# Turning the inverted chunk rows back while VectorE still works on them, with unread wide products on TensorE in two stages of a four-block kernel

## The chip, the cores and the metric

The kernel runs on one core of a Trainium2 chip. The metric is the device time of one execution in microseconds, the median of several runs. All data are 32-bit floats.

## The reference, cut to what matters

The reference is a chain of four blocks over 4096 tokens of 128 channels (16 sequences of 256): an attention with decays, a two-of-eight expert layer, a delta-rule attention, and a one-of-eight expert layer, each followed by a layer norm over the sum with its input. The change lies in the third block, in its projections and in the inverse of its chunks:

```python
q, k, v = silu(causal_conv(hs @ Wq)), silu(causal_conv(hs @ Wk)), silu(causal_conv(hs @ Wv))
q, k = l2norm(q), l2norm(k)                      # 4 heads of 32 channels
k_beta = k * sigmoid(hs @ Wb)
A = where(strict_lower, -(k_beta @ k.T), 0)      # 32x32, per head and chunk of 32 tokens
for i in range(1, 32):
    row = A[i]
    A[i] = row + row @ A
T = A + eye(32)
u, w = T @ v, T @ k_beta                         # then a scan over the 8 chunks of a sequence
local_long = depthwise_fir(v, firl)              # 63 taps
```

## The kernel before, in words

The program is a row of stages; between most of them all engines meet. The third block is `delta_project`, `delta_invert` and `gate_stage`. The engines run their own instruction lists and wait on semaphores.

`delta_project` takes 8 groups of 512 tokens. For each group TensorE (PE) turns four tiles of normalized rows into channel-major form (L1381, and L1430 for group 0), makes the projections with their convolution as 128x512 products (`convolve`, L1386; the projections of v and of beta, L1398 and L1402), sums squares by head (L1409), and multiplies keys with keys and queries in 128 products of 32x32 by 64 columns (L1422, "scores"). Work is staged one and two groups ahead. In the last group nothing is ahead, so PE has only the square sums and, once VectorE (DVE) has made `kq` (L1644, semaphore `s_kq`), the scores; DVE then masks them into `A` and `attn` (L1576). At the stage's start PE's first instruction is the turning of group 0, tile by tile as DVE normalizes it.

`delta_invert` has all 512 chunk matrices (128 chunks of 4 heads) at once. PE turns `A` so that the 128 partitions are the chunks (32 transposes of 128x128, L1698), ScalarE (ACT) copies them into `M[chunk, row, head, column]` in 8 groups of 4 rows (L1731). DVE then substitutes column by column, for j from 1 to 30:

```python
tmp = M[:, j+1:32, hh, j] * M[:, j, hh, 0:j]     # L1761, two pairs of heads
M[:, j+1:32, hh, 0:j] += tmp                     # L1768
```

These are 4 instructions a step, 120 in all, each of which raises `s_dve` by one. Row i no longer changes after step i-1. While DVE works, PE computes the long FIR in 768 products of 32x32 (L1711), which ACT copies out in 8 parts (L1734, semaphore `s_fc`). After the last step DVE sets the four diagonals to 1 (L1773) and raises `s_done`; PE waits for `s_done`, turns the 32 rows of `M` back (L1721), four to a PSUM bank, and ACT copies the 8 banks over `A` (L1744, semaphore `s_U`), after which `gate_stage` starts with products of 32x32 (L1982, L2013) and copies on GpSimd (POOL, L2213). PE may use a bank again when the copy before has left it (`s_U` at k-3). Between the FIR's copies and L1744, ACT loads two tables and makes three small activations (L1737 to L1740).

Of the kernel before, what the change touches and what calls it, by code (L numbers as in the profile page):

```python
# [22 lines left out]
P = 128  # L23
# [6 lines left out]
NG = TOK // GTOK  # L30
# [1244 lines left out]
def delta_project(nc, sem, keep, x_parts, xT_out, v_rows, s_rows, tables, w):  # L1275
# [10 lines left out]
    with ctx:  # L1286
# [3 lines left out]
        C, wqkv, wb, taps, tapr, fir = (tables[n] for n in ("C", "wqkv", "wb", "taps", "tapr", "fir"))  # L1290
# [22 lines left out]
        B = [ctx.enter_context(nc.psum_tensor(f"c_bank{i}", [P, GTOK], F32))[:, :] for i in range(8)]  # L1313

        def s(name):
            return sem("delta_" + name)

        s_set, s_x, s_out = s("constants_set"), [s("rows_in_0"), s("rows_in_1")], s("rows_out")
        s_T, s_xT, s_p, s_pad, s_beta = s("transposed"), s("channel_major"), s("projected"), s("padded"), s("beta")
# [4 lines left out]
        s_ln, s_dve, s_blk, s_wc = s("logarithms"), s("vector_steps"), s("value_blocks"), s("weights_by_tap")  # L1324
# [3 lines left out]
        block = ctx.enter_context(nc.Block())  # L1328
# [44 lines left out]
        @block.tensor  # L1373
        def _(pe):
            mm = nc.tensor.matmul

            def turn_rows(m):
                pe.wait_ge(s_xT, m)
                for t in range(GT):
                    pe.wait_ge(s_xn, 4 * m + t + 1)  # L1380
                    i = nc.tensor.transpose(B[0][:, t * P:(t + 1) * P], xn[:, t, :], C["ident"])  # L1381
                i.then_inc(s_T, 1)

            def convolve(k):
                for j in range(4):
                    i = mm(B[1 + k].rearrange("p (s t) -> p s t", s=GSEQ), wc[:, k, j, :], xT[:, :, j:SEQ + j],  # L1386
                           start=(j == 0), stop=(j == 3))
                i.then_inc(s_p, 1)

            def project(m, first=False):  # L1390

                rows = xT[:, :, 3:SEQ + 3]
                out = lambda b: B[b].rearrange("p (s t) -> p s t", s=GSEQ)
                pe.wait_ge(s_xT, m + 1)
                convolve(0)
                if not first:
                    pe.wait_ge(s_pad, m)
                mm(out(3), wqkv[:, 2, :], rows, start=True, stop=True).then_inc(s_p, 1)  # L1398
                convolve(1)
                if not first:  # L1400
                    pe.wait_ge(s_beta, m)
                mm(out(4), wb[:], rows, start=True, stop=True).then_inc(s_p, 1)  # L1402

            def step(n, b, r, first, last):
                if not first:
                    pe.wait_ge(s_ln, 2 * n)
                for k in range(2):
                    pe.wait_ge(s_sq, 2 * n + k + 1)
                    mm(B[5 + k], C["same32"], sq[k][:], start=True, stop=True).then_inc(s_ss, 1)  # L1409
                if not first:  # L1410
                    pe.wait_ge(s_m, 2 * n)
                if not last:
                    project(n + 1)
                if ahead(n, 2):
                    turn_rows(n + 2)
                pe.wait_ge(s_kq, n + 1)
                if not last:
                    pe.wait_ge(s_act, 3 * n + 5)
                for c in range(GTOK // 32):
                    for h in range(4):  # L1420
                        rows = slice(32 * h, 32 * h + 32)
                        i = mm(B[1 + c // NCH][rows, (c % NCH) * 64:(c % NCH) * 64 + 64], kn[rows, 32 * c:32 * c + 32],  # L1422
                               kq[rows, c].rearrange("p k c -> p (k c)"), start=True, stop=True,
                               skip_group_check=True)
                    if c % NCH == NCH - 1:
                        i.then_inc(s_sc, 1)

            for t in range(GT):
                pe.wait_ge(s_xn, t + 1)
                i = nc.tensor.transpose(B[0][:, t * P:(t + 1) * P], xn[:, t, :], C["ident"])  # L1430
            i.then_inc(s_T, 1)
            pe.wait_ge(s_wc, 1)
            project(0, first=True)
            turn_rows(1)
            steps(pe, step)
# [221 lines left out]
def delta_invert(nc, sem, keep, l_rows, later, loads):  # L1657
# [4 lines left out]
    with ctx:  # L1662
# [3 lines left out]
        C, toe = {"ident": keep["ident"][:]}, keep["toe"]  # L1666
# [6 lines left out]
        def s(name):  # L1673
            return sem("invert_" + name)

        s_fir, s_fc, s_out, s_later = s("fir"), s("fir_copied"), s("fir_out"), s("gate_weights_in")
        s_at, s_M, s_done, s_ut, s_U, s_dve = s("chunks_transposed"), s("chunk_rows"), s("inverted"), s("back_transposed"), s("kept"), s("vector_steps")
        block = ctx.enter_context(nc.Block())

        @block.sync  # L1680
        def _(sp):
            for dst, src in loads:
                sp.dma_start(dst, src).then_inc(s_later, 16)
            sp.wait_ge(s_fc, 8)
            sp.dma_start(l_rows, fir[:].rearrange("p m c -> p (m c)")).then_inc(s_out, 16)
            sp.wait_ge(s_out, 16)
            sp.wait_ge(keep["value_blocks"], 16)

        @block.tensor
        def _(pe):  # L1690
            mm = nc.tensor.matmul
            A = keep["A"][:].rearrange("p n s c -> p (n s) c")
            V = keep["v"][:].rearrange("p n s c -> p (n s) c")
            for c in range(32):
                k = c // 4
                if c % 4 == 0 and k >= 4:
                    pe.wait_ge(s_M, k - 3)
                i = nc.tensor.transpose(Q[k % 4][:, (c % 4) * P:(c % 4 + 1) * P], A[:, :, c], C["ident"])  # L1698
                if c % 4 == 3:
                    i.then_inc(s_at, 1)  # L1700

            pe.wait_ge(keep["toeplitz_in"], 16)
            for k in range(8):
                if k >= 4:
                    pe.wait_ge(s_fc, k - 3)
                for j in range(4):
                    c = 4 * k + j
                    for lag in range(LAGS):
                        for h in range(4):
                            rows = slice(32 * h, 32 * h + 32)  # L1710
                            i = mm(R[k % 4][rows, j * P + lag * NSEQ:(j + 1) * P], toe[rows, c, lag, :],  # L1711
                                   V[rows, 0:P - lag * NSEQ, c],
                                   start=(j == 0 and lag == 0), stop=(lag == LAGS - 1), skip_group_check=True)
                i.then_inc(s_fir, 1)
            pe.wait_ge(s_done, 1)
            for c in range(32):
                k = c // 4
                pe.wait_ge(s_M, 8)
                if c % 4 == 0 and k >= 4:
                    pe.wait_ge(s_U, k - 3)  # L1720
                i = nc.tensor.transpose(Q[k % 4][:, (c % 4) * P:(c % 4 + 1) * P],  # L1721
                                        M[:, c].rearrange("p h j -> p (h j)"), C["ident"])
                if c % 4 == 3:
                    i.then_inc(s_ut, 1)
# [21 lines left out]
        @block.vector  # L1746
        def _(dve):
            v = nc.vector
            dve.wait_ge(s_M, 8)
            done = [0, 0]  # L1750
            own = Steps(s_dve)


            for j in range(1, 31):
                rows = 31 - j
                for pair in range(2):
                    hh = slice(2 * pair, 2 * pair + 2)
                    t = tmp[pair][:, 0:rows * 2 * j].rearrange("p (i h c) -> p i h c", h=2, c=j)
                    if done[pair]:
                        dve.wait_ge(s_dve, done[pair])  # L1760
                    done[pair] = own.mark(v.tensor_tensor(t, M[:, j + 1:32, hh, j:j + 1].broadcast_to([P, rows, 2, j]),  # L1761
                                                 M[:, j:j + 1, hh, 0:j].broadcast_to([P, rows, 2, j]), ALU.mult))
                for pair in range(2):
                    hh = slice(2 * pair, 2 * pair + 2)
                    out = M[:, j + 1:32, hh, 0:j]
                    t = tmp[pair][:, 0:rows * 2 * j].rearrange("p (i h c) -> p i h c", h=2, c=j)
                    dve.wait_ge(s_dve, done[pair])
                    done[pair] = own.mark(v.tensor_tensor(out, out, t, ALU.add))  # L1768
            dve.wait_ge(s_dve, done[1])
            flat = M[:].rearrange("p i h c -> p (i h c)")  # L1770
            for h in range(4):

                i = v.memset(flat[:, h * 32:h * 32 + 31 * 129 + 1:129], 1.0)  # L1773
            i.then_inc(s_done, 1)


def gate_tables(nc, ctx, w, consts, route):
# [1005 lines left out]
```

## Time and profile before

| | |
|---|---|
| median of 3 runs | 1081.73 us (1079.55 to 1085.17) |
| the profiled execution | 1084.69 us, span 1082.9 us |
| busy share PE, DVE, ACT, POOL | 83%, 68%, 51%, 41% |
| mean granted TensorE clock | 0.894 |
| `delta_project` | about 514 to 657 us |
| `delta_invert` | about 657 to 722 us |

A row of the timeline gives start and duration in us from the span's start, the engine, the line, the operation with what it writes and reads, how many instructions were merged, and in brackets how long the engine was idle before and what ended it. PEld is the weight load of TensorE. In a row of windows the busy time (and number of instructions) of PE, PEld, DVE, ACT and POOL is followed by the granted TensorE clock as a share of 2.4 GHz, the DMA share and GB/s. 0.50 is 1.2 GHz and 1.00 is 2.4 GHz.

### The profile page before, as it was taken

The numbers are of one execution on the slowest core, as the hardware profiler recorded it, in microseconds if no ns is written. First come the engines' busy times: TensorE is split into PE (matmuls) and PEld (weight loads), VectorE is DVE, ScalarE is ACT, GpSimd is POOL, SyncE is SP. The second block draws the span as 40 slices with busy tenths as digits, with TensorE's granted clock in tenths as the row PEclk, the third lists the DMA queues.
The fourth block names the chain that finished last, engine by engine and source line by source line (L and its number), as shares of the span: only waits on it lengthen the run. The fifth ranks groups of instructions, "written<-read, shape, count | busy, mean of one in ns | idle before, by whom it ended". The sixth has DMA issues, their size and how long they took to land. (4 is left out here: it accounts for less than half of the span.)

```text
span 1082.9 us, 34100 instructions
## 1 busy us (share of the span) xinstructions
PE 897.5 (83%) x12739; PEld 642.8 (59%) x12740; DVE 741.6 (68%) x2235; ACT 551.0 (51%) x1103; POOL 444.0 (41%) x576
## 2 busy tenths in 40 slices
PE   7899999999853999996689878849899997519995
PEld 4567666666633888886244437647566663218884
DVE  3778898887543555554588896943689997745664
ACT  1477666666311455543377772333565555316663
POOL 1001333444463445444376640011134544655776
PEclk7899999999965999999699997956899997658998
DMA  3112221153012311111443215123112225012110
GB/s 93 21 41 51 58 54 48 50 187 102 24 50 79 86 53 57 56 55 31 105 101 88 60 31 171 45 74 103 42 52 59 64 72 195 13 50 51 54 54 22
DMA packets 122053, 73.14 MB, mean 68 GB/s; under 512 B 63299, under 2 KB 108457, under 8 KB 121536
## 3 DMA queue, kind: packets, MB, share of 16 engines
q1 hardware_dynamic: 113648, 57.80, 19.8%
q0 software_dynamic: 6592, 12.70, 3.4%
q8 instruction: 93, 1.52, 0.6%
q10 hardware_dynamic: 1680, 0.80, 0.3%
q14 instruction: 40, 0.33, 0.1%
HBM read 42.69 MB, written 27.38 MB: 65 GB/s over the span
## 5 line engine op out<-in xcount | busy, mean ns | idle before, releaser
L1181 ACT ACTIVATE bx_h<-bx_up,bx_cur 128x128 f32<-128x128 f32 x284 | 81.0, 369 | 104.9 <-PE bx_up L1152 98.7
L1110 POOL DMA_INDIRECT chosen_b<-bx_ys,bx_to x71 | 73.6, 1037 | 97.8 <-DVE bx_ys L1224 69.1
L601 POOL DMA_INDIRECT regions_b<-a_xo,a_seat x64 | 65.2, 1019 | 88.7 <-ACT a_at L715 69.6
L715 ACT ACTIVATE a_at<-a_scores 128x1024 f32<-128x1024 f32 x64 | 65.6, 1025 | 69.9 <-PE a_scores L469 63.0
L1152 PE MATMUL bx_up<-bx_xT,bx_cur 128*128 128x128 f32 x568 | 81.3, 287 | 5.5 <-DVE bx_cur L1197 3.9
L1134 PE MATMUL bx_down<-bk_w,bx_h 128*128 x568 | 80.8, 285 | 3.2 <-ACT bx_h L1181 3.2
L1152 PEld LDWEIGHTS bx_up<-bx_xT,bx_cur 128*128 128x128 f32 x568 | 70.3, 195 | 15.2 <-DVE bx_cur L1197 9.5
L1134 PEld LDWEIGHTS bx_down<-bk_w,bx_h 128*128 128x128 f32 x568 | 68.8, 191 | 6.6 <-issue 3.7
L1197 DVE TENSOR_SCALAR bx_cur<-bk_w 128x516 f32 x71 | 30.6, 431 | 53.4 <-issue 49.7
L1386 PE MATMUL c_bank<-c_xT,c_wc 128*128 128x512 f32 x128 | 62.1, 630 | 4.8 <-DVE keep_attn L1576 4.0
L464 PE MATMUL a_scores<-a_rk,a_kx 32*128 32x128 f32 (+3 forms) x1024 | 56.8, 293 | 8.8 <-DVE a_at L928 6.3
L464 PEld LDWEIGHTS a_scores<-a_rk,a_kx 32*128 32x128 f32 x1024 | 42.1, 189 | 35.8 <-DVE a_at L928 27.4
L608 POOL TENSOR_SCALAR a_vr<-a_mv 128x4 f32<-128x4 f32 x8 | 1.9, 242 | 133.8 <-DVE a_mv L867 133.7
L469 PE MATMUL a_scores<-a_rk,a_kx 32*128 32x32 f32 (+3 forms) x1024 | 55.1, 276 | 1.3 <-issue 1.3
L928 DVE COPY_PREDICATED a_at<-a_earlier,a_scores 128x256 f32<-128x256 uint32 x64 | 28.1, 440 | 35.9 <-ACT a_at L715 35.0
L1386 PEld LDWEIGHTS c_bank<-c_xT,c_wc 128*128 128x128 f32 x128 | 25.3, 200 | 39.5 <-issue 32.1
L2213 POOL COPY g_kak<-keep_k 128x512 f32<-128x512 f32 x16 | 9.9, 620 | 93.6 <-POOLq L2731 68.7
L1152 PE MATMUL dx_up<-dx_xT,dx_cur 128*128 128x128 f32 x312 | 46.4, 294 | 0.8 <-issue 0.6
L1170 ACT ACTIVATE dx_cur<-space 128x516 f32 x39 | 24.7, 633 | 41.5 <-ACT dx_h L1181 22.2
L1134 PE MATMUL dx_down<-space,dx_h 128*128 x312 | 45.6, 290 | 0.2 <-ACT dx_h L1181 0.2
L1110 POOL DMA_INDIRECT out_rows<-dx_ys,dx_to x39 | 42.4, 1088 | 7.9 <-issue 7.9
L1181 ACT ACTIVATE dx_h<-dx_up,dx_cur 128x128 f32<-128x128 f32 x156 | 43.9, 363 | 3.2 <-PE dx_up L1152 3.2
(450 smaller groups left out, 2492.8 us busy)
## 6 DMA issues: line engine op xcount, KB each, us to landing
bx_xs<-regions_b SPq DMA_DIRECT2D x72, 65.0 KB, 1.9
bk_w<-in_b_w SPq DMA_DIRECT2D x16, 256.0 KB
space<-in_d_w SPq DMA_DIRECT2D x16, 256.0 KB
c_part<-chosen_b SPq DMA_DIRECT2D x15, 256.0 KB
dx_xs<-regions_d SPq DMA_DIRECT2D x40, 65.0 KB, 1.9
a_xp<-in_a_xT SPq DMA_DIRECT2D x8, 256.0 KB
a_xr<-in_x SPq DMA_DIRECT2D x8, 256.0 KB
lion_values<-a_vt SPq DMA_DIRECT2D x8, 256.0 KB
```

The costliest lines, as they stand in the source:

```text
L464: mm(S4[:, g, o:o + P - 32 * q], kx[rows, 0, 4 * t + q].rearrange("p h j -> p (h j)"), rk[b][rows, 0, t * P + 32 * q:(t + 1) * P], start=T ...
L469: i = mm(S4[:, g, o + P - 32 * q:o + P + 32], kx[rows, 1, 4 * t + q].rearrange("p h j -> p (h j)"), rk[b][rows, 2, t * P:t * P + 32 * q + 32],
L601: nc.gpsimd.indirect_dma_start(route["regions"], bass.IndirectOffsetOnAxis(ap=seat[b][:, k, t:t + 1], axis=0), xo[b][k][:, t, :], None).th ...
L715: op(at[m % 2][:], S4[:, :, 0:320].rearrange("p g (q k) -> p g q k", q=2)[:, :, :, 0:P], ACT.Copy).then_inc(s_ata, 1)
L928: v.copy_predicated(at[m % 2][:, :, :, 0:32], earlier[:].unsqueeze(1).unsqueeze(1).broadcast_to([P, 4, 2, 32]), later).then_inc(s_atd, 1)
L1110: nc.gpsimd.indirect_dma_start(dest, bass.IndirectOffsetOnAxis(ap=to[u][:, 0:1], axis=0), ys[u][:], None, bounds_check=dest.shape[0] - 1, ...
L1134: i = mm(BY[u % 2][:, 0:P], h[u % 2][:, f, :], w2[:, bass.ds(e, 1), f, :].rearrange("p e c -> p (e c)"), start=(f == 0), stop=(f == FC - 1))
L1152: i = mm(BU[u % 2][:, f * P:(f + 1) * P], cur[u % 2][:, f * P:(f + 1) * P], xT[u % 2][:], start=True, stop=True)
L1170: op(cur[u % 2][:], w1[:, bass.ds(e, 1), :].rearrange("p e c -> p (e c)"), ACT.Copy).then_inc(s_cur, 1)
L1181: i = op(h[u % 2][:, f, :], BU[u % 2][:, f * P:(f + 1) * P], act_fn, bias=cur[u % 2][:, FC * P + f:FC * P + f + 1])
L1197: v.tensor_scalar(cur[u % 2][:], w1[:, bass.ds(e, 1), :].rearrange("p e c -> p (e c)"), 1.0, None, ALU.mult).then_inc(s_cur, 1)
L1386: i = mm(B[1 + k].rearrange("p (s t) -> p s t", s=GSEQ), wc[:, k, j, :], xT[:, :, j:SEQ + j], start=(j == 0), stop=(j == 3))
```

## The change

In `delta_invert`:

- the wait of PE for `s_done` goes. PE waits instead for `s_diag` 4 (the diagonals) and `s_fc` 8 (all FIR copies), and ahead of group k of the turned rows for `s_dve` at 4(4k+2): 8, 24, 40, 56, 72, 88, 104 and 120. The wait for `s_U` at k-3 stays.
- the diagonals are set by GpSimd, in four memsets of 128x32, once ACT has filled `M`.
- ahead of groups 5, 6 and 7 PE makes 3, 6 and 4 products of 128x128 by 512 columns into `R[0]`, a FIR bank that nobody reads any more.

In `delta_project`:

- ahead of group 0's turning PE makes 12 products of 128x128 by 384 columns into bank 3, without any wait.
- in the last group, between the square sums and the scores, PE waits for `s_pad` 8 and makes 16 such products into bank 3.

What these products write is never read.

```diff
+            def keep_busy(out, k):
+                weights = wqkv[:].rearrange("p k c -> p (k c)")
+                for _ in range(k):
+                    mm(out[:, 0:3 * P], C["ident"], weights, start=True, stop=True, skip_group_check=True)
...
+                if last:
+                    pe.wait_ge(s_pad, NG)
+                    keep_busy(B[3], 16)
                 pe.wait_ge(s_kq, n + 1)
...
+            keep_busy(B[3], 12)
             for t in range(GT):
                 pe.wait_ge(s_xn, t + 1)
...
+            v_row = keep["v"][:].rearrange("p n s c -> p (n s c)")[:, 0:512]
+            def keep_busy(out, k):
+                for _ in range(k):
+                    mm(out, C["ident"], v_row, start=True, stop=True, skip_group_check=True)
...
-            pe.wait_ge(s_done, 1)
+            pe.wait_ge(s_diag, 4)
+            pe.wait_ge(s_fc, 8)
             for c in range(32):
                 k = c // 4
-                pe.wait_ge(s_M, 8)
-                if c % 4 == 0 and k >= 4:
-                    pe.wait_ge(s_U, k - 3)
+                if c % 4 == 0:
+                    keep_busy(R[0], (0, 0, 0, 0, 0, 3, 6, 4)[k])
+                    pe.wait_ge(s_dve, 4 * (4 * k + 2))
+                    if k >= 4:
+                        pe.wait_ge(s_U, k - 3)
...
-            dve.wait_ge(s_dve, done[1])
+        @block.gpsimd
+        def _(pool):
+            pool.wait_ge(s_M, 8)
             flat = M[:].rearrange("p i h c -> p (i h c)")
             for h in range(4):
-                i = v.memset(flat[:, h * 32:h * 32 + 31 * 129 + 1:129], 1.0)
-            i.then_inc(s_done, 1)
+                nc.gpsimd.memset(flat[:, h * 32:h * 32 + 31 * 129 + 1:129], 1.0).then_inc(s_diag, 1)
```

## Rows read from the trace of the kernel before

**Rows 1.** First line of the profile's page.
```profile
span 1082.9 us, 34100 instructions
```

**Rows 2.** Busy time by windows, the inverse before and after the FIR's end.
```profile
662.70:699.50 36.80, 36.71 (x770) 26.62 (x768) 35.89 (x80) 8.43 (x10) 0.00 (x0) 1.00 0.06 13
699.50:713.90 14.40, 0.05 (x1) 0.05 (x1) 14.20 (x45) 4.08 (x6) 0.00 (x0) 0.59 0.34 146
```

**Rows 3.** Timeline, end of the inverse.
```profile
699.48 1.03 ACT L1734 ACTIVATE i_fir<-i_fir 128x512 f32<-128x512 f32 x1 [3.52 <-PE i_fir L1711]
...
703.42 0.20 ACT L1740 ACTIVATE g_itc<-g_temp 128x4 f32<-128x4 f32 x1
...
707.05 0.84 DVE L1761 TENSOR_TENSOR i_tmp<-i_M 128x300 f32<-128x300 f32 x2
...
709.25 0.76 DVE L1768 TENSOR_TENSOR i_M<-i_M,i_tmp 128x260 f32<-128x260 f32 x2
...
713.10 0.34 DVE L1768 TENSOR_TENSOR i_M<-i_M,i_tmp 128x60 f32<-128x60 f32 x2
...
713.85 6.29 PE L1721 MATMUL i_bank<-c_ident,i_M 128*128 128x128 f32 x32 [14.44 <-DVE i_M L1773]
715.01 7.17 ACT L1744 ACTIVATE space<-i_bank 128x512 f32<-128x512 f32 x8 [11.38 <-PE i_bank L1721]
...
723.49 1.93 PE L1982 MATMUL g_wu_xy<-space 32*32 32x64 f32 x64 [3.35 <-PEq L2731]
```

**Rows 4.** Timeline, start of the inverse.
```profile
657.17 5.65 PE L1698 MATMUL i_bank<-c_ident,space 128*128 128x128 f32 x32 [1.14 <-PEq L1286]
...
660.86 2.72 ACT L1731 ACTIVATE i_M<-i_bank 128x512 f32<-128x512 f32 x5 [0.26 <-PE i_bank L1698]
...
663.61 0.42 DVE L1761 TENSOR_TENSOR i_tmp<-i_M 128x60 f32<-128x60 f32 x2 [6.76 <-ACT i_M L1731]
...
668.57 0.84 DVE L1761 TENSOR_TENSOR i_tmp<-i_M 128x300 f32<-128x300 f32 x2
```

**Rows 5.** PE's transposes by windows (PE busy, clock, DMA share, GB/s).
```profile
714.00:719.00 5.00, 5.00 (x24) 0.50 0.00 0
661.20:662.40 1.20, 1.20 (x13) 1.00 0.67 231
```

**Rows 6.** Windows where the granted clock falls and rises in the inverse.
```profile
702.00:702.50 0.50, 0.00 (x0) 0.00 (x0) 0.50 (x2) 0.49 (x3) 0.00 (x0) 0.60 0.84 360
...
719.00:719.50 0.50, 0.50 (x6) 0.50 (x5) 0.00 (x0) 0.50 (x2) 0.00 (x0) 0.83 0.00 0
```

**Rows 7.** Timeline, last two groups of the projection.
```profile
627.58 0.80 DVE L1592 TENSOR_SCALAR c_cv<-c_pad,c_taps 128x512 f32<-128x512 f32 x1
...
641.04 0.45 DVE L1592 TENSOR_SCALAR c_cv<-c_pad,c_taps 128x512 f32<-128x512 f32 x1
...
641.36 1.99 PE L1422 MATMUL c_bank<-c_kq,c_kn 32*32 32x64 f32 x128
...
652.40 3.63 PE L1422 MATMUL c_bank<-c_kq,c_kn 32*32 32x64 f32 x128 [7.13 <-DVE c_kq L1644]
...
653.39 0.67 DVE L1648 STREAM_TRANSPOSE c_hs<-c_vb 128x512 f32<-128x512 f32 x1
...
656.43 0.42 DVE L1576 TENSOR_TENSOR keep_attn<-c_bank,c_con 128x256 f32<-128x256 f32 x1
```

**Rows 8.** Window of PE's idle time in the projection's last group.
```profile
645.30:652.40 7.10, 0.00 (x1) 0.03 (x1) 5.98 (x12) 4.98 (x7) 1.13 (x2) 0.65 0.34 63
```

**Rows 9.** Timeline, start of the projection.
```profile
514.15 0.10 POOL L1439 MEMSET c_eps<- 128x1 f32 x1 [3.18 <-POOLq L2731]
...
523.32 0.48 PE L1430 MATMUL c_bank<-c_con,c_xn 128*128 128x128 f32 x1 [15.11 <-DVE c_xn L1613]
...
526.42 5.30 PE L1386 MATMUL c_bank<-c_xT,c_wc 128*128 128x512 f32 x6 [0.78 <-ACT c_xT L1505]
...
533.28 3.60 PE L1386 MATMUL c_bank<-c_xT,c_wc 128*128 128x512 f32 x8
```

More of the change, by code:

```diff
@@ L1676, in delta_invert @@
         s_fir, s_fc, s_out, s_later = s("fir"), s("fir_copied"), s("fir_out"), s("gate_weights_in")
-        s_at, s_M, s_done, s_ut, s_U, s_dve = s("chunks_transposed"), s("chunk_rows"), s("inverted"), s("back_transposed"), s("kept"), s("vector_steps")
+        s_at, s_M, s_diag, s_ut, s_U, s_dve = s("chunks_transposed"), s("chunk_rows"), s("diagonals_set"), s("back_transposed"), s("kept"), s("vector_steps")
         block = ctx.enter_context(nc.Block())
```

## Prediction

> **What bounds the kernel now.** The kernel is a row of stages with meetings of all engines between them, so I read it by stage. The page gives the span, 1082.9 us [rows 1]; the profiled execution took 1084.69 us, 1.8 us more than its span and 3.0 us more than the median of the three runs (1081.73). The sum below is made against 1084.69 and then taken off the median. Next I read the windows of the inverse, then its timeline, for what ends last there.
>
> The windows show two halves. Up to 699.5 us PE computes the FIR (36.71 of 36.80 us busy, clock 1.00) beside DVE's steps; from 699.5 to 713.9 DVE alone is busy (14.20 of 14.40 us), PE does nothing and its clock falls (mean 0.59) [rows 2]. In the timeline the last step ends at 713.10 + 0.34 = 713.44; after the diagonals PE starts its 32 transposes at 713.85, ACT's first copy starts at 715.01 and the eighth ends at 715.01 + 7.17 = 722.18; the next stage starts at 723.49 [rows 3]. From 713.44 to 722.18, 8.7 us, only PE and ACT work, on rows of which seven eighths were final before. That tail is fully on the path: every engine meets behind it. DVE's steps are the path before it (663.61 to 713.44 [rows 3, 4]), and before them lie ACT's copies, PE's transposes, and the scores and masks of the projection's last group, where PE had been idle for 7.1 us and its clock had fallen (mean 0.65) [rows 7, 8].
>
> Of the clock: four rows of `M` of 128 columns each are turned in 24 transposes per 5.00 us at 0.50, so 0.21 us each, and 13 in 1.20 us at 1.00, about 0.10 [rows 5]. A product of 512 columns at 1.00 is repeated every (3.60 - 0.6) / 7 = 0.43 us [rows 9], at 0.50 four times 0.21 = 0.85; 384 columns are three quarters of that: 0.32 and 0.64 us. The 128 scores take 1.99 us at full and 3.63 at half clock [rows 7].
>
> **The tail of the inverse.** Removed: the wait for the last step ahead of groups 0 to 6. Group 7 still waits for it (`s_dve` 120). What has to come after 713.44 is then four transposes and one copy. From PE's start to ACT's start the trace shows 1.16 us at half clock [rows 3]; at full clock it is less by about half of four transposes, some 0.7. A copy is repeated every 7.17 / 8 = 0.9 us and the last takes about 1.07. So the end comes at 713.44 + 0.05 + 0.7 + 1.07 = 715.3 in place of 722.18: a gain of 6.9 us (6.4 if the clock is low). I take 6.9.
>
> This holds only if groups 0 to 6 and the 13 wide products are done by 713.44. PE can start at 699.48 + 1.03 = 700.5 (`s_fc` 8) and turns groups 0 to 3 by about 702.3. ACT isn't free for copies before its tables and small activations end at 703.42 + 0.20 = 703.6 [rows 3]; its first copy lets PE into group 4 at about 704.6. From there PE has 12 transposes (groups 4 to 6) and 13 wide products ahead of group 7: at full clock 12 x 0.1 + 13 x 0.43 = 6.8 us, done at 711.4; step 26, for which group 6 waits, ends at 709.25 + 0.76 = 710.0 [rows 3] and is no hindrance. The clock will most likely fall once on the way: in the trace it fell at about 702.1, 2.7 us after the FIR, with PE idle [rows 6], and here PE is idle from 702.3 to 704.6. It rises again when PE works without a break: it rose at about 719.2, 5.3 us after the transposes began at 713.85 [rows 3, 6], and was up at 661.2, 4.0 us after those at 657.17 [rows 4, 5]. PE would lose half of some 4.0 to 5.3 us, 2.0 to 2.7, and be ready for group 7 at 713.4 to 714.1. So the stall is nothing to 0.7 us, and I take none, since part of that stretch may lie before the fall. With no rise at all it is the rival below. Which engine is late next: ACT, with group 6 copied by about 712.6, isn't; then DVE's last step is the only thing that group 7 waits for.
>
> A rule speaks against that recovery. First the row: the 32 transposes were alone on PE from 713.85, and in them the clock went from 0.50 to 1.00 at 719.2 [rows 5, 6]. The Trainium skill, "TensorE: Matmul & The Clock Gate", Part 4, says that transposes don't count as activity for the clock as other products do, and that full clock isn't granted for them. By that rule the last four transposes would run at half clock and the tail would gain 6.4 and not 6.9; the trace disagrees with the rule, and I keep 6.9.
>
> **The diagonals.** DVE loses four memsets, in the 0.41 us between 713.44 and 713.85, counted above. GpSimd, idle in this stage, makes four at the start of DVE's steps; its one memset of the trace takes 0.10 us [rows 9], so some 0.4 us in all, hidden behind 50 us of steps; PE waits for `s_diag` only at 700.5. If GpSimd disturbs DVE meanwhile, the nearest row is one DVE instruction that took 0.45 us in one group and 0.80 in another [rows 7]: 0.4 us of overlap costs at most 0.3. I take 0.
>
> **Other traffic during the last steps.** New beside steps 14 to 30 are PE's reads of `M` and ACT's copies into `A`. DVE's instruction of 300 elements takes 0.42 us (0.84 for two) at 668.57 with PE's FIR beside it and 0.42 at 707.05 with PE idle [rows 3, 4], so PE's reads cost DVE nothing. I take 0; the upper bound is a rival.
>
> **The last group of the projection.** PE ends its square sums at 645.3 [rows 8], and `s_pad` 8 comes from ACT's copy of group 7's projection, made before the squares that PE has just summed. The 16 products take 16 x 0.32 = 5.1 us at the full clock that PE has there (the mean of 0.65 over the 7.1 us from 645.3 is 2.1 us at 1.00 and 5.0 at 0.50, a fall at about 647.5 [rows 8]) and end at 650.5, 1.9 us before `kq` is ready at 652.40 [rows 7]. They delay nobody. After idle times of 2.2 us (645.3 to 647.5) and 2.7 us (699.4 to 702.1) the clock fell; 1.9 us is a little less, so I take it that the scores run at full clock: 1.99 in place of 3.63, 1.6 us. The masks after them end at 656.43 + 0.42 = 656.85 now; with all scores there by 654.4 they are DVE's own four of 0.35 each, begun when its transposes end at 653.39 + 0.67 = 654.06 [rows 7], done at 655.5. That gives 1.35 us. From the first transpose of `A` that follows to the last of ACT's eight copies it is 663.58 - 657.17 = 6.4 us; at full clock the first copy starts after some 0.7 us and ACT alone paces them, 2.72 / 5 = 0.54 each [rows 4], so 0.7 + 8 x 0.54 = 5.0 to 5.4 with some waiting, 1.0 us or a little more less. Between 0 and 1.0 I take 0.5, since the pause between the stages (some 1.4 us) can lose the clock again. Part sum: 1.85; bounds 0 and 2.35.
>
> **The start of the projection.** PE is free from about 514.2 [rows 9]. The 12 products begin at half clock and end between 514.2 + 12 x 0.64 = 521.9 at the latest and about 520; the first tile to turn is there at 523.32, so they delay nothing. They could save if the clock stayed up: six convolution products are at half clock from 526.42 [rows 9], 0.42 us each, 2.5 us. But from 520 to 522 until 526.42 PE has only four transposes (about 1 us of work in 4.5 to 6.5 us), more idle time than the 2.2 and 2.7 us after which the clock fell. I take 0; bounds 0 and 2.5.
>
> **The next stage.** Its first products (L1982, L2013) run at half clock now [rows 3]. PE will have ended 2.6 us before it starts (713.9 to about 716.6), which by the same rows is about where the clock falls. I take 0; the rival below prices the other.
>
> **Sum.** 6.9 + 1.85 = 8.75 us: 1084.69 becomes 1075.9, and the median 1081.73 becomes 1073.0.
>
> **Rivals.**
>
> *The clock is kept into the next stage or through the projection's start.* The idle times there are near the ones after which it fell. In the next stage the first 128 products are covered by GpSimd's copies; behind them two rounds of about 3.6 us would take half: some 3.2 us more, 1069.8. For: 2.6 us of pause against falls at 2.2 and 2.7. Against: two falls after such pauses, and no hold. Chance 0.16.
>
> *The projection's products bring nothing*, because the clock is lost in the 1.9 us before the scores. Then the tail alone is left: 1081.73 - 6.9 = 1074.8. For: 1.9 is close to 2.2. Chance 0.17.
>
> *DVE is slowed in its last steps* by GpSimd, PE or ACT beside it. If the instructions after 700.5 grew as 0.45 grew to 0.80 [rows 7], 13 us would become 23 and the gain would be gone, about 1083; a growth by a quarter leaves 1076.2. Against: the pair of rows with and without the FIR is equal. Chance 0.05, around 1077.
>
> *Slower: the wide products stay at half clock and stand in the way.* Place: PE's list ahead of the scores and of group 7. Price: 16 x 0.64 = 10.2 us from 645.3 ends at 655.6, so the scores come 3.2 us late and still take 3.63. In the inverse, from 704.6, 12 x 0.21 + 13 x 0.85 = 13.6 us leads to 718.2, then 1.16 and 1.07: 720.4, only 1.7 us earlier than 722.18. Together +1.5 us, 1083.2. It decides from a 384-column product of over (7.1 + 1.7) / 16 = 0.55 us; at full clock it is 0.32. Against: PE comes to the 16 straight from work at 1.00. Chance 0.02.
>
> **How the numbers follow.** Forecast 0.60; the rivals 0.16, 0.17, 0.05 and 0.02. The likeliest is 1073.0. The range holds the tail alone with a small stall or a slow copy (1077) and the kept clock (1069.5); runs of the kernel before differ by 5.6 us among themselves, so I take 1069.0 to 1077.5. A difference under 0.5% (5.4 us) can't be told from no change here; faster by more means under 1076.3. That takes the forecast, the two rivals of 1069.8 and 1074.8 nearly whole: 0.86. Within: 0.12. Slower: 0.02.
>
> **What would show it.** Right: L1744 as eight copies spread over about 704 to 715.5 with only the last behind the last step; 32 transposes of L1721 of which only four start after it; the next stage about 8.7 us earlier, near 714.8; scores of the last group in 2.0 us. Wrong: group 7's transposes starting more than 0.3 us after the last step (wide products late), DVE's 300-element pair over 0.84 us, the scores beginning after `kq`, or the 12 first products followed by convolutions at 1.00 at 526.4.

## The result, and the profile after

The changed kernel's median is 1079.47 us (20 runs, 1071.19 to 1084.15) beside 1084.10 us for the kernel before (20 runs, 1078.27 to 1089.05): a ratio of 0.9958, 95% interval 0.9940 to 0.9976. It is faster by 4.6 us, 0.4%. Forecast were 8.75 us and a range of 1069.0 to 1077.5. The direction was right and the size was not. Part of the distance to the range is the base it was laid from: 1081.73 us, the median of three runs, where 20 runs gave 1084.10. The ratio taken off 1081.73 would be 1077.2; the gain of 4.6 for 8.75 us falls short by itself. The profiled execution took 1082.90 us (span 1081.1). Executions more than 1.5% above the fastest of their kernel are left out of the ratios; there are two, both of the kernel with 16 products in the last group alone, and its profiled one (1094.71 us) is among them.

Three places of the timeline after answer to [rows 9], [rows 7] and [rows 3]. First the start of the projection:

```profile
513.94 10.77 PE L1388 MATMUL c_bank<-c_wqkv,c_con 128*128 128x384 f32 x24 [5.99 <-PEq L2752]
...
524.55 1.14 PE L1440 MATMUL c_bank<-c_con,c_xn 128*128 128x128 f32 x4
...
526.47 3.67 PE L1392 MATMUL c_bank<-c_xT,c_wc 128*128 128x512 f32 x8 [0.78 <-ACT c_xT L1515]
```

Twelve products stand there as 24 matmul instructions. They hold PE until 524.5, about when the four tiles are ready to turn, not until 520 to 522, and the convolutions run at full clock: eight in 3.67 us, where six took 5.30 at half clock [rows 9].

The same in the projection's last group:

```profile
642.87 10.59 PE L1388 MATMUL c_bank<-c_wqkv,c_con 128*128 128x384 f32 x32 [0.20 <-DVE keep_attn L1586]
...
648.97 0.68 DVE L1654 TENSOR_TENSOR c_kq<-c_kn,c_beta 128x512 f32<-128x512 f32 x1
...
653.39 1.99 PE L1431 MATMUL c_bank<-c_kq,c_kn 32*32 32x64 f32 x128
...
654.55 0.42 DVE L1586 TENSOR_TENSOR space<-c_bank,c_con 128x256 f32<-128x256 f32 x1 [3.09 <-PE c_bank L1431]
```

Sixteen products are 32 instructions, 10.59 us instead of the 5.1 forecast. `kq` is ready at 649.65, so the scores, at 653.39, are over 3 us late; DVE waits 3.09 us for them. They do run at full clock (1.99 us).

And the end of the inverse:

```profile
709.13 5.32 PE L1708 MATMUL i_fir<-keep_v,c_ident 128*128 128x512 f32 x12
...
712.42 0.33 DVE L1788 TENSOR_TENSOR i_M<-i_M,i_tmp 128x60 f32<-128x60 f32 x2
...
714.29 0.60 PE L1741 MATMUL i_bank<-c_ident,i_M 128*128 128x128 f32 x4
714.72 3.60 PE L1708 MATMUL i_fir<-keep_v,c_ident 128*128 128x512 f32 x8
...
718.16 0.60 PE L1741 MATMUL i_bank<-c_ident,i_M 128*128 128x128 f32 x4
...
718.80 1.02 ACT L1764 ACTIVATE space<-i_bank 128x512 f32<-128x512 f32 x1 [2.82 <-PE i_bank L1741]
...
721.16 1.93 PE L2003 MATMUL g_wu_xy<-space 32*32 32x64 f32 x64 [2.40 <-PEq L2752]
```

DVE's last step ends at 712.75. Group 6 is turned only at 714.3 and group 7 at 718.2, because 12 and 8 wide instructions stand ahead of them. From 704.1 to 707.3 PE worked on them at half clock, which cost some 1.6 us and which the forecast had allowed for. The last copy ends at 719.82, 7.1 us after the last step. Before, with everything still to turn, it was 8.7 [rows 3]; forecast was 1.8.

By stages, from one profile each (us):

| kernel | projection, to the first transpose of `A` | to DVE's first step | steps | last step to the next stage | next stage, to the expert layer |
|---|---|---|---|---|---|
| before | 142.8 | 6.4 | 49.8 | 10.1 | 249.9 |
| changed | 142.4 | 6.4 | 49.8 | 8.4 | 250.9 |
| no products | 142.5 | 6.6 | 49.8 | 3.6 | 249.7 |
| start 12 alone | 139.8 | 4.8 | 49.8 | 10.1 | 243.3 |
| end 16 alone | 144.1 | 4.8 | 49.8 | 10.1 | 259.5 |
| end 8 alone | 141.5 | 4.8 | 49.8 | 10.1 | 239.4 |
| inverse 13 alone | 143.3 | 6.7 | 49.8 | 8.5 | 241.1 |
| start 6 alone | 143.1 | 6.7 | 49.8 | 10.0 | 242.8 |
| 12, 8, none | 138.9 | 4.8 | 49.8 | 3.5 | 249.0 |
| 12, 8, 2+3+2 | 138.7 | 4.8 | 49.8 | 3.2 | 242.6 |
| 12, 16, 13 at half width | 138.7 | 4.8 | 49.8 | 3.1 | 242.7 |
| 12, 8, 2+3+2 and 2 behind | 138.8 | 4.8 | 49.8 | 3.8 | 241.1 |
| 10, 10, 2+3+2 | 139.0 | 4.8 | 49.8 | 3.1 | 241.6 |

The last column differs by 12 us among the kept executions, and by 20 with the one that was left out, in a stage that no kernel here changes. One profile can't tell what a change brings in all; totals are read only from many runs. The first four columns can be read, the first of them to some tenths: it is 142.5 to 143.3 in the three kernels that leave the projection alone. The four columns of the changed kernel sum to 207.0 us beside 209.1 before.

Its 6.4 us to DVE's first step are as long as before, though the transposes of `A` are at full clock. PE's timeline shows why:

```profile
656.52 2.71 PE L1715 MATMUL i_bank<-c_ident,space 128*128 128x128 f32 x22 [1.14 <-PEq L1286]
660.88 1.28 PE L1715 MATMUL i_bank<-c_ident,space 128*128 128x128 f32 x10 [1.65 <-issue]
```

Between two transposes PE stood for 1.65 us and waited for nothing that the profile names ("issue"). No other kernel of this study with the clock up there has that pause (4.8 us in the table). What it is stays open, and so does whether other executions of the changed kernel have it.

### The profile page after: what moved, and what is told of

It is laid out like the page before. It is cut to its first block and busy times, and to the rows that moved or that the text cites. A ratio compares the mean times of both kernels' runs of the same rounds, so it can differ in the third digit from the quotient of the medians.

```text
span 1081.1 us, 34264 instructions
## 1 busy us (share of the span) xinstructions
PE 923.4 (85%) x12821; PEld 655.0 (61%) x12822; DVE 741.2 (69%) x2231; ACT 550.3 (51%) x1103; POOL 445.6 (41%) x580
## 5 line engine op out<-in xcount | busy, mean ns | idle before, releaser
L1392 PE MATMUL c_bank<-c_xT,c_wc 128*128 128x512 f32 x128 | 57.9, 594 | 7.8 <-DVE keep_attn L1586 7.0
L489 PE MATMUL a_y_bank<-a_at,a_vx 128*32 128x128 f32 (+3 forms) x1024 | 42.6, 256 | 3.4 <-issue 3.3
```

The lines of the kernel that those rows point to most:

```text
L489: i = mm(Y[32 * g:32 * g + 32, t * P + 32 * q:(t + 1) * P], by_group(vx[b][:, 4 * t + q, :])[:, g, :], at[m % 2][:, g, q % 2, 0:k], start= ...
```

## The experiments

Theory A: one `matmul` call on these operands is two matmul instructions, so the unread products last twice as long as forecast and stand in the way of the scores and of groups 6 and 7. Its rivals are named with the runs. The kernels are run against the kernel before on the same chip; on the first chip that had a median of 1081.71 us, on the others 1059.08 and 1059.61, so only ratios are compared.

**No products.** The groups are turned one by one and GpSimd sets the diagonals; nothing else is left.

```diff
-                if last:
-                    pe.wait_ge(s_pad, NG)
-                    keep_busy(B[3], 16)
...
-            keep_busy(B[3], 12)
...
-                    keep_busy(R[0], (0, 0, 0, 0, 0, 3, 6, 4)[k])
```

> The change with all unread products taken out (12, 16 and 3+6+4): only the rows turned back group by group and the diagonals by GpSimd are left. Theory A (each float32 product is two matmul instructions, so the 13 wide products held group 7 back by 5.0 us in the changed kernel): here group 7's first transpose starts within 0.3 us of DVE's last step, and from the first transpose of A to the next stage's first product it is 66.3 - 6.5 = 59.8 us (66.3 before, 64.6 with the change). Rival B (the turned groups are bound by ACT's copies or PE's order, not by the products): it stays near 64. Rival C (what is won is given back in the next stage by its clock): 59.8 here, but a total less than 3 us under the kernel before. A without C: 6 us under it.

Ratio 0.9937 (0.9911 to 0.9963), 6.8 us. PE and DVE at the end of the inverse:

```profile
712.13 1.11 PE L1736 MATMUL i_bank<-c_ident,i_M 128*128 128x128 f32 x4 [2.32 <-DVE i_M L1783]
```

```profile
711.74 0.33 DVE L1783 TENSOR_TENSOR i_M<-i_M,i_tmp 128x60 f32<-128x60 f32 x2
```

The last step ends at 712.07 and PE follows in 0.06 us: the wait is now the last step, as forecast. From the first transpose of `A` to the next stage it is 60.0 us (59.8 expected). Rivals B and C fall. The clock is low here, and the tail gains 6.5 us (10.05 less 3.55) beside the 6.4 that the forecast gave for that case. So this part alone is worth more than the whole change: by the stages clearly (202.5 beside 207.0 us up to the next stage), by the totals only by their middles, since the intervals overlap.

**The start alone**, in the kernel before.

> The kernel before with only the 12 products of 384 columns ahead of group 0's turning. Theory A: they are 24 instructions, fill PE from 513.9 to about 524.5, the clock is 1.00 at the first convolution, and the projection is 2.6 us shorter; the total falls by about 2.6 us. Rival: the 2.6 us are met later by a transfer or by DVE, the total is unchanged.

Ratio 0.9965 (0.9936 to 0.9995), 3.8 us; the projection takes 139.8 us, 3.0 less. The rival of an unchanged total lies just outside the interval. DVE's first step also came 1.7 us sooner after the transposes of `A` began, with no product added near them:

```profile
651.00:652.00 1.00, 0.03 (x1) 0.06 (x1) 0.65 (x2) 0.00 (x0) 0.00 (x0) 0.94 1.03 430
```

PE's clock was up again just ahead of its transposes at 651.97, after scores at half clock (3.64 us). In the kernel before, the same scores were followed by half clock until 661.1, 3.9 us into the transposes [rows 4, 5]. So a like gain there can come without products; why it came here stays open.

**The last group alone, 16 products.**

> The kernel before with only the 16 products of 384 columns in the last group. Theory A: 32 instructions of 0.32 us end 10.5 us after the square sums, the scores start 1.0 us later than before but at full clock (1.99 for 3.63 us), the transposes of A too; the next 1.0 to 1.5 us come back there: DVE's first step is within 1.0 us of where it was, total within 1 us of before. Rival (they keep PE busy and cost nothing): 1.9 us faster.

Ratio 1.0021 (0.9993 to 1.0050). The profile is read for the projection alone:

```profile
645.77 10.59 PE L1388 MATMUL c_bank<-c_wqkv,c_con 128*128 128x384 f32 x32 [0.19 <-DVE keep_attn L1585]
656.29 1.99 PE L1431 MATMUL c_bank<-c_kq,c_kn 32*32 32x64 f32 x128
```

Counted from the stage's start the scores come 3.0 us later than before, not 1.0 as expected. 142.8 + 6.4 becomes 144.1 + 4.8: what the clock gives back in the transposes of `A` is what the late scores cost. Two microseconds faster is excluded.

**The last group alone, 8 products.**

> The kernel before with only 8 products of 384 columns in the last group. Theory A: 16 instructions end 5.2 us after the square sums, 1.4 to 1.9 us ahead of kq; the scores take 2.0 us, DVE's first step comes 1.35 + 1.6 = 3.0 us earlier, total 3 us under before, where 16 products gave nothing or a loss. Rival (the clock is lost in the pause ahead of the scores): 3.6 us for the scores, no change of the total.

```profile
626.60 5.43 PE L1388 MATMUL c_bank<-c_wqkv,c_con 128*128 128x384 f32 x16 [0.20 <-DVE keep_attn L1585]
633.45 1.99 PE L1431 MATMUL c_bank<-c_kq,c_kn 32*32 32x64 f32 x128 [1.42 <-DVE c_kq L1653]
636.82 3.38 PE L1707 MATMUL i_bank<-c_ident,space 128*128 128x128 f32 x28 [1.39 <-PEq L1286]
```

The products now take 5.4 us, about the 5.1 that the forecast gave to sixteen; PE waits 1.42 us for `kq`, and scores and transposes stay at full clock. The stretch is 146.3 us, 2.9 less, as expected. The total is 0.9987 (0.9967 to 1.0008): 1.4 us by its middle, with both the expected 3 us and no gain inside the interval. So the gain of this part is shown in the stage, not in the total. Whether the clock is lost in that pause in some executions, one profile doesn't tell.

**The inverse alone, 13 products.**

> The change's inverse alone, with its 13 products, no products in the projection. Theory A (26 instructions of 0.43 us, or 0.85 where the clock is low, between groups 5 and 7): group 7 starts 4 to 6 us after the last step, the stage from its first transpose to the next stage's is 64 to 66 us (60.0 without the products), total 0 to 3 us under before and 4 us over the kernel with no products (1075.5). Rival (they give back in the next stage by its clock what they cost): the same stage, but the total within 1 us of 1075.5.

```profile
692.77 5.32 PE L1704 MATMUL i_fir<-keep_v,c_ident 128*128 128x512 f32 x12
697.92 0.60 PE L1737 MATMUL i_bank<-c_ident,i_M 128*128 128x128 f32 x4
698.36 3.60 PE L1704 MATMUL i_fir<-keep_v,c_ident 128*128 128x512 f32 x8
701.79 0.60 PE L1737 MATMUL i_bank<-c_ident,i_M 128*128 128x128 f32 x4
```

The last step ends at 696.3 and group 7 is turned at 701.8. Ratio 0.9975 (0.9958 to 0.9992), 2.6 us, beside 0.9937 without products: by the middles the 13 products cost 4 us of 6.8, by the table 5.0 of 6.5. The next stage does start with the clock up here (its first 64 instructions take 1.09 us), and that doesn't pay for them.

**12, 8 and 2+3+2 products**, the whole change with about half the work in the two places where it was late.

```diff
-                    keep_busy(B[3], 16)
+                    keep_busy(B[3], 8)
...
-                    keep_busy(R[0], (0, 0, 0, 0, 0, 3, 6, 4)[k])
+                    keep_busy(R[0], (0, 0, 0, 0, 0, 2, 3, 2)[k])
```

> The change with 12, 8 and 2+3+2 products in place of 12, 16 and 3+6+4. Theory A: the scores begin when kq is ready, group 7 when DVE's last step ends; the next stage starts 2.6 + 1.9 + 6.9 = 11.4 us earlier than in the kernel before (2.3 with the change), total 9 to 11 us under before. Rival C (given back in the next stage): the next stage's start as said, but the total less than 6 us under before. Rival (half the products lose the clock): scores 3.6 us again, start 9 us earlier.

Ratio 0.9855 (0.9824 to 0.9887): 15.7 us, and 1065.07 us is the lowest median on that chip.

```profile
704.80 1.88 PE L1708 MATMUL i_fir<-keep_v,c_ident 128*128 128x512 f32 x4
706.52 0.60 PE L1741 MATMUL i_bank<-c_ident,i_M 128*128 128x128 f32 x4
709.50 1.09 PE L2003 MATMUL g_wu_xy<-space 32*32 32x64 f32 x64 [2.37 <-PEq L2752]
```

The last step ends at 706.35 and group 7 starts 0.17 us later; the next stage comes 3.2 us after the step. The tail is 3.15 us for 10.05, the gain of 6.9 that the prediction took for full clock. Up to that point 12.6 us are gained against the kernel before by the table (196.5 beside 209.1), 1.2 us more than expected; the transposes of `A` kept their clock, of which the expectation counted only a part. The total passed the expected 9 to 11 us (the interval is 12.2 to 19.0). The rest of the 15.7 lies in the next stage and can't be told from its scatter.

**The same counts at half the width**: 192 columns for the 16, 256 for the 13.

> The change with its counts (12, 16, 3+6+4) but 192 columns in place of 384 for the 16 and 256 in place of 512 for the 13. Theory A (the loss is PE's time in these products): as with half the counts, the scores begin when kq is ready and group 7 when the last step ends; ratio to before 0.985 to 0.989. Rival E (the loss is one of the number of products, or of the bank and the waits they stand between): scores still 1 us late and group 7 still 4 us late, ratio 0.995.

Ratio 0.9860 (0.9829 to 0.9890), and the stages are those of half the counts (138.7, 4.8, 3.1); PE waits 1.38 us for `kq`, and group 7 is turned 0.06 us after the last step. What costs is the time for which the products hold PE, not their number or their place in the list. Rival E falls.

**6 products at the start**, which is the length that the prediction gave to 12.

> The kernel before with only 6 products of 384 columns at the projection's start, the length that the prediction gave to 12. Its step was: they end at 520 to 522, the clock falls in the pause before the first convolution, nothing is won. If that step was right for that length: 12 instructions, end at 519 to 520, first convolutions at 0.50, the projection 142.8 us as before. Rival (any warm-up is enough): 140.0 us as with 12 products, total 2.6 us under before.

Ratio 0.9995 (0.9976 to 1.0014), projection 143.1 us. PE's timeline, and a window over the first convolutions:

```profile
498.38 6.33 PE L1388 MATMUL c_bank<-c_wqkv,c_con 128*128 128x384 f32 x12 [5.76 <-PEq L2738]
507.64 0.33 PE L1437 MATMUL c_bank<-c_con,c_xn 128*128 128x128 f32 x1 [2.94 <-DVE c_xn L1620]
```

```profile
511.00:513.00 2.00, 2.00 (x3) 0.76 (x3) 0.00 (x0) 1.66 (x3) 1.49 (x2) 0.50 0.47 85
```

With nearly 3 us of pause and a thin row of transposes behind the products, the clock is at half at the convolutions. The step of the forecast was right for the length that it assumed.

**12, 8 and none in the inverse**, and **two more products behind group 7** of the 2+3+2 kernel.

> The change with 12 products at the start, 8 in the last group and none in the inverse. Theory D (a shorter list of wide products in the inverse is worth something in itself: the clock is 1.00 when group 7 is turned and is carried into the next stage): group 7's copy starts about 0.5 us later than with 2+3+2, the next stage's first 128 products take 3.6 us and not 2.0, total 3 to 6 us over the kernel with 2+3+2 (1065.07). Rival (products in the inverse are worth nothing, all is in not being late): within 2 us of 1065.

> The kernel with 12, 8 and 2+3+2 products, with 2 more unread products of 512 columns behind group 7's transposes, while ACT copies its bank. Theory D (the next stage begins at the clock that PE left with): they take 1.7 us of the pause of 2.6 us and delay nobody; the next stage's products stay at 1.00 for longer, total 0 to 4 us under 1065. Rival (the stage's clock is set by its own small products): no difference.

Ratios 0.9904 (0.9880 to 0.9928) and 0.9875 (0.9856 to 0.9893), side by side on one chip. The products in the inverse are thus worth about 3 us by the middles once they are late for nothing; the two intervals overlap. Their timelines begin the next stage so:

```profile
694.58 1.93 PE L2002 MATMUL g_wu_xy<-space 32*32 32x64 f32 x64 [2.37 <-PEq L2751]
```

```profile
693.11 1.09 PE L2004 MATMUL g_wu_xy<-space 32*32 32x64 f32 x64 [1.30 <-PEq L2753]
```

That is half clock without them and full clock with them, as the theory said; without them the clock had fallen before the last transposes. But products in the inverse don't settle it: the changed kernel has 13 of them, and behind the same pause as with 2+3+2 (2.40 and 2.37 us) it starts the stage at half clock. The row is the pause, between group 7's transposes and the stage:

```profile
718.80:721.10 2.30, 0.00 (x0) 0.00 (x0) 0.00 (x0) 1.02 (x1) 0.00 (x0) 0.97 0.00 0
```

Its clock fell at about 721.0, 0.2 us before the stage began. In the kernel with the inverse and its 13 products alone it fell 1.1 us after the stage began (705.8), with 2+3+2 5.7 us after (715.2). So what is carried over depends on when the fall comes, and these traces don't show what sets that moment. The tail's own two products can't be told from none in the total: 2+3+2 alone started the stage at full clock too, and 0.9875 lies within the interval of 0.9855. They weren't free, as the expectation had it: the next stage came 3.8 us after the last step instead of 3.2.

**10, 10 and 2+3+2.**

> The best guess from the runs so far: 10 products at the start, 10 in the last group, 2+3+2 in the inverse. 20 instructions end at about 523, just ahead of the first tile to turn; 20 of 0.32 us in the last group end 6.5 us after the square sums, 0.5 us ahead of kq. If the fit is all that counts it equals the kernel with 12, 8 and 2+3+2 (0.9855 of before) within 0.3%.

Ratio 0.9888 (0.9850 to 0.9925), the same stages to 0.3 us (139.0, 4.8, 3.1). The middles lie 0.33% apart, about the 0.3% that was allowed, and the intervals overlap, so it can't be told from 12 and 8. As far as these runs resolve it, the exact count doesn't matter as long as nothing is late and no long pause is left.

## Why the prediction was wrong

**The step that failed** is the price of a wide product: "A product of 512 columns at 1.00 is repeated every (3.60 - 0.6) / 7 = 0.43 us [rows 9]". The row is right for an instruction, and the change was counted in calls. The code in front of it has four calls a convolution, two convolutions and 8 groups, 64 calls, and the page lists L1386 128 times; L1398 stands twice a group with one call. Filler of the same kind was in the kernel before, in its first stage, where 9 calls of `keep_busy` stand as 18 instructions:

```profile
1.75 6.13 PE L353 MATMUL a_free<-a_ones 128*128 128x256 f32 x18 [1.75 <-POOL a_maa_w L591]
```

The "128 products" of the scores are 64 calls in the same way, and the 768 of the FIR are 384. That was to be read before pricing. The 41 calls added are 82 instructions, which the page of the changed kernel also shows: 12821 on PE beside 12739. The transposes do stand once for each call, and for those the counting was right.

**The tail.** Forecast 6.9 us; 1.7 measured in the profile, since group 7 waited 5.4 us for the products. Without them it is 6.5 us in the table at half clock (6.4 forecast) and 6.8 in runs, and with 2+3+2 at full clock 6.9 in the table (6.9 forecast). So the mechanism was right, its pricing too, and "done at 711.4" was the error.

**The last group.** Forecast +1.85 us. The scores did run at full clock, but over 3 us late; alone it is 0.3 us gained in the profile and 2.3 (-0.8 to 5.4) lost in runs. With 8 products the forecast's description holds step by step, and the stretch gains 2.9 us.

**The start.** Forecast 0 with bounds of 0 and 2.5. It gained 2.3 us in the changed kernel's profile (DVE's masks of the last group but one ended at 642.8 instead of 645.4, in a stage that began 0.2 us sooner) and 3.8 us (0.5 to 6.9) alone. The pause of the argument "more idle time than the 2.2 and 2.7 us after which the clock fell" wasn't there: the 24 instructions fill it. Six calls show the pause and no gain.

**The sum.** The product of the ratios of the three parts alone, 0.9965 x 1.0021 x 0.9975, is 0.9961; measured were 0.9958. So close a match is in part luck, since each interval is 0.3% to 0.6% wide. By the table the parts give 4.6, 0.3 and 0.8 us up to the next stage, 5.7 together, and the changed kernel 2.1. Of the difference 1.7 us are the transposes of `A` at full clock, which two of the parts gain and the whole can gain only once, and 1.6 the unnamed pause in them.

**The rivals.** The slower one named the right place and mechanism: products in PE's list ahead of the scores and of group 7. It took half clock for what would stretch them, and its point of decision, 0.55 us for a product of 384 columns, was passed (two times 0.32 at full clock). It came out faster all the same, since the start gained what it had not been given, and since the scores, once late, were at full clock. The rival of the kept clock and the forecast of the last group both rested on pauses of 2.2 and 2.7 us after which the clock fell. The traces don't give one such length: in the projection's last group it fell 2.2 us after the square sums in the kernel before, and 4.2 us after them (at 644.3) in the one with the start alone, and behind pauses of 2.4 us the next stage began at half clock in the changed kernel, whose clock had been up until then, and at full clock in four others. DVE wasn't slowed by GpSimd, PE or ACT: the steps are 49.8 us in all kernels. The diagonals on GpSimd took 0.16 us each, 0.34 together, and hid behind the first step (the row is of the kernel with 12, 8 and 2+3+2):

```profile
656.53 0.34 POOL L1795 MEMSET i_M<- 128x32 f32 x4 [5.75 <-ACT i_M L1751]
```

The rule of the Trainium skill, "TensorE: Matmul & The Clock Gate", Part 4, that full clock doesn't engage for transposes, weighed in the prediction, is not put to a test of its own by any of these runs.

## What to carry to other kernels

Count instructions, not calls: before pricing an added operation, divide the profile's count of a like line by the calls in the code. Filler work in an engine's own list has two edges: too little leaves a pause in which the clock is lost (6 calls at the start: nothing gained), too much delays the instruction behind it (16 in the last group: the gain gone). Take its length from the measured wait. And keep the parts of a change apart: here the part without filler was worth more than the whole.

## What the runs showed of the hardware

A product with float32 operands of 128x128 by 512 columns is two instructions of 0.43 us at full clock, 0.86 us in all; 128-column transposes of float32 are one of 0.1. The clock fell in pauses of PE, but not after one fixed length of them: at one and the same place it was 2.2 us in one trace and 4.2 in another.

The stage behind the inverse took from 239.4 to 250.9 us in kept executions of kernels that don't touch it, and 259.5 in the one left out. Windows with PE busy throughout show the clock at half there for many microseconds. The first row is of the changed kernel, the second of the left-out execution of the kernel with 16 products alone:

```profile
864.00:872.00 8.00, 8.00 (x141) 5.48 (x140) 7.34 (x24) 2.88 (x6) 5.05 (x6) 0.57 0.25 68
```

```profile
840.00:850.00 10.00, 10.00 (x183) 8.18 (x177) 8.45 (x25) 1.37 (x3) 4.48 (x8) 0.50 0.11 36
```

In the kernel before, 890 to 900 us is at half clock too, with PE busy for 9.31 of 10.00 us. In such a stretch PE does in ten microseconds what takes about five at full clock, so two or three of them, or none, would make the 11 to 13 us that lie between the fastest and slowest run of the two kernels; that is argued, not shown. What sets them off stays open.
